# Attention scores in half-array F32R tiles, causal masks in the same halves, and a new schedule for the maximum pass

## The reference, cut to what matters

```
q = q * cos + rotate_half(q) * sin          # k likewise
scores = einsum('bhqd,bhkd->bhqk', q, k) / sqrt(16)
scores = where(causal, -inf, scores)
attn = softmax(scores)                      # maximum of each query is subtracted
out = einsum('bhqk,bhkd->bhqd', attn, v)
```

## Time and profile before

| what | us |
|---|---|
| device time, median of 3 runs | 2709.79 |
| span of the profiled execution, first to last instruction | 2663.3 |
| projection | 367.9 |
| routing | 44.8 |
| first two steps' maximum jobs | 23.5 |
| first pass of the attention loop | 852.7 |
| second pass | 858.1 |
| experts and dense | 516.0 |

### The profile page before, as it was taken

How to read it: one execution, slowest core, us unless ns; L and a number is a source line. 1 busy time by engine, 2 the same in 40 slices (tenths; PEclk the granted TensorE clock), 3 DMA queues, 4 the chain that set the end, 5 groups by cost and what they waited for, 6 DMA issues and landing times. The chain is left out here.

```text
span 2663.3 us, 49751 instructions
## 1 busy us (share of the span) xinstructions
PE 2394.4 (90%) x14968; PEld 1211.4 (45%) x14968; DVE 2072.5 (78%) x3856; ACT 1463.1 (55%) x1762; POOL 377.9 (14%) x319
## 2 busy tenths in 40 slices
PE   0999947999999999998899999999999868886998
PEld 0889942333333333232333333333322247776888
DVE  7888889999999988562799999988864257776776
ACT  2444513566666666777566666666677733332443
POOL 2111149500000000000000000000000023333344
PEclk9999977999999999999999999999999979998999
DMA  4122247300000021000410000003100144443232
GB/s 123 64 95 91 90 114 186 104 9 9 9 9 1 9 50 43 13 10 17 92 30 9 9 9 9 1 9 70 28 9 9 22 115 126 126 126 97 64 95 71
DMA packets 158629, 144.79 MB, mean 54 GB/s; under 512 B 36448, under 2 KB 142176, under 8 KB 158304
## 3 DMA queue, kind: packets, MB, share of 16 engines
q1 hardware_dynamic: 155360, 133.94, 18.9%
q0 software_dynamic: 3072, 8.39, 0.9%
HBM read 95.61 MB, written 46.66 MB: 53 GB/s over the span
## 5 line engine op out<-in xcount | busy, mean ns | idle before, releaser
L883 DVE TENSOR_REDUCE attn_MX<-psB 128x1 f32<-128x512 f32 (+3 forms) x2352 | 1357.2, 638 | 352.5 <-PE psB L756 223.2
L869 ACT ACTIVATE attn_PB<-psB 128x1024 f32<-128x1024 f32 (+3 forms) x1152 | 1035.8, 950 | 563.9 <-PE psB L788 509.7
L756 PE MATMUL psB<-attn_KS,attn_QS 96*128 96x512 bf16 (+3 forms) x2352 | 764.5, 370 | 51.5 <-DVE attn_MX L883 44.9
L788 PE MATMUL psB<-attn_QS,attn_KS 104*128 104x512 bf16 (+3 forms) x2304 | 652.6, 363 | 24.5 <-ACT attn_QS L846 16.0
L803 PE MATMUL psB<-attn_PB,attn_V 128*32 128x512 f32 (+3 forms) x4608 | 579.8, 570 | 0.0
L756 PEld LDWEIGHTS psB<-attn_KS,attn_QS 96*128 96x128 bf16 x2352 | 200.6, 97 | 639.8 <-DVE attn_MX L883 522.2
L788 PEld LDWEIGHTS psB<-attn_QS,attn_KS 104*128 104x128 bf16 x2304 | 210.2, 98 | 336.1 <-ACT attn_PB L869 128.9
L1043 POOL TENSOR_TENSOR W1L<-W,W1H 128x512 fp32r<-128x512 f32 x36 | 53.8, 1524 | 1664.3 <-ACT W1H L1120 1664.3
L803 PEld LDWEIGHTS psB<-attn_PB,attn_V 128*32 128x32 f32 x4608 | 96.3, 108 | 175.9 <-issue 166.8
L759 PE MATMUL psB<-attn_mask_qk,attn_idb 128*128 128x128 bf16 x544 | 119.2, 227 | 0.0
L42 PE MATMUL ps_experts<-W2H,HH_experts 128*128 128x256 f32 x256 | 83.9, 328 | 35.1 <-DVE Y_experts L1233 20.3
(11 more groups left out here) (213 smaller groups left out, 3216.5 us busy)
## 6 DMA issues: line engine op xcount, KB each, us to landing
W<-in_w SPq DMA_DIRECT2D x18, 1024.0 KB, 5.5
attn_KS<-qk_parts SPq DMA_DIRECT2D x240, 64.0 KB, 3.7
attn_QS<-qk_parts SPq DMA_DIRECT2D x210, 64.0 KB, 2.8
qk_parts<-proj_PT SPq DMA_DIRECT2D x32, 384.0 KB, 3.3
attn_V<-v_rows SPq DMA_DIRECT2D x40, 256.0 KB, 4.8
v_rows<-proj_VA SPq DMA_DIRECT2D x32, 256.0 KB, 2.0
XI_experts<-rows_by_place SPq DMA_DIRECT2D x9, 512.0 KB, 6.3
AO_experts<-attention_sums SPq DMA_DIRECT2D x9, 512.0 KB, 6.7
```

The source lines that it names most:

```text
L756: mm = nc.tensor.matmul(ps[:, bank, 0:width], QS[0:MROW, i % 4, h, j * P:(j + 1) * P], KS[w][0:MROW, h, kc * CH:kc * CH + width], start=Tr ...
L788: mm = nc.tensor.matmul(ps[:, bank, r * P:CH], KS[w][0:KROWS, h, kb * P:(kb + 1) * P], QS[0:KROWS, i % 4, h, r * P:CH], start=True, stop=( ...
L869: nc.scalar.activation(PB[:, u % RING, 2 * pair:2 * pair + 2, r * P:CH], ps[:, 2 * (s % 2):2 * (s % 2) + 2, r * P:CH], ACT.Exp, scale=HD * ...
L883: nc.vector.tensor_reduce(MX[:, m % 4, HG * j + h, kc:kc + 1], ps[:, MB + off % 3, 0:w], AX.X, ALU.max).then_inc(reduced, 1)
```

## The change

It changes these things and nothing else.

- **Parts.** q and k are cut into two F32R parts instead of three bf16 parts. Lines 277, 343 and 280 become one subtraction. `qk_parts` is [2, 512, 4096] float32.
- **Layout.** A head's contraction is 52 rows: high x high, high x low (16 rows each), 4 rows for the maximum, low x high. Heads 0 and 2 of a group lie in partitions 0 to 51, heads 1 and 3 in 64 to 115. The key and query tiles are F32R, with two heads on the free axis. All score products and maximum jobs run on 64 rows of the array; a score pair is one product in each half, into different banks.
- **Masks.** The mask product becomes two products of 64 columns for each head, 64 rows deep, in the head's own half (`later_qk`, `later_kq` times `hide`).
- **Maximum pass.** The diagonal jobs of the first two query blocks (one block in c = 0) take two heads at once into one bank, with one reduction. Diagonal jobs are issued in twos: both products, then the masks of both. A pass has 1092 jobs, 1152 before. `max_pass_pace` draws the smoothest line between the number of jobs that must be done and the number that may be done at each unit, and follows it.
- **Constants and loads.** The rows of ones come by 8 DMAs from a small tile instead of from GpSimd's 48 operations. A query load is 8 DMAs (two set the maximum rows to zero), before 6. SyncE waits for two small memsets first. `max_rows` has 8 small products, before 4.
- The first score pair of a step waits for both of ScalarE's `rows` copies.

```diff
-        PT = sb("PT", [P, 4, 3, CH], BF16)
-        RS = sb("RS", [P, 2, CH])
+        PT = sb("PT", [P, 4, 2, CH], F32R)
...
+                        dve.wait_ge(high_made, 4 * c + u + 1)
+                        nc.vector.tensor_tensor(PT[:, u, 1, :], ps[:, QTB + u % 2, :], PT[:, u, 0, :].bitcast(F32),
+                                                ALU.subtract).then_inc(low_made, 1)
...
-PAIRS = ((0, 0), (0, 1), (1, 0), (1, 1), (0, 2), (2, 0))
-MROW = HD * len(PAIRS)
-KROWS = MROW + 2 * HG
+TILE = P // 2
+MROW, MROWS = 32, 4
+TERMS = ((0, 0, 0), (HD, 0, 1), (MROW + MROWS, 1, 0))
+KROWS = HD * len(TERMS) + MROWS
...
+def diagonal_jobs(c):
+    paired = TPC // 2 if c > 0 else 1
+    wide = [(j, (t, t + 2), c) for j in range(paired) for t in range(2)]
+    return wide + [(j, (h,), c) for j in range(paired, TPC) for h in range(HG)]
...
-PACE = 4.5
-            room = min(room, 1.0) + PACE * (TPC - r) / TPC
-            while at < end(i + 1 + AHEAD) and room >= cost[at]:
...
+    path, at = [work[end(AHEAD)]], 0
+    while at < len(order):
+        low, high, low_at, high_at = float("-inf"), float("inf"), at, at
+        for to in range(at + 1, len(when)):
+            span = when[to] - when[at]
+            floor, roof = (work[least[to]] - path[at]) / span, (work[most[to]] - path[at]) / span
+            if floor > high or roof < low:
+                break
+            if floor >= low:
+                low, low_at = floor, to
+            if roof <= high:
+                high, high_at = roof, to
+        turn, slope = (high_at, high) if floor > high else (low_at, low)
+        path += [path[at] + slope * (when[to] - when[at]) for to in range(at + 1, turn + 1)]
+        at = turn
...
+                    for at, h in enumerate(hs):
+                        rows, b = slice(TILE * (h % 2), TILE * (h % 2) + KROWS), h // 2
+                        mm = nc.tensor.matmul(ps[:, bank, at * width:(at + 1) * width], QS[rows, i % 4, b, j * P:(j + 1) * P],
+                                              KS[w][rows, b, kc * CH:kc * CH + width], start=(at == 0), stop=(kc < c))
...
+                    both = jobs[i % LS][at:at + 2]
+                    for n, job in enumerate(both):
+                        max_job(reads, i, off + n, job, used(n), q_need)
+                    for half in range(2):
+                        for n, job in enumerate(both):
+                            mm = hide_later_keys(off + n, job, half)
+                            if half == 1:
+                                mm.then_inc(maxed, 1)
...
+                    for t in range(2):
+                        rows = slice(TILE * t, TILE * t + KROWS)
+                        mm = nc.tensor.matmul(ps[:, 2 * (s % 2) + t, r * P:CH], KS[w][rows, pair, kb * P:(kb + 1) * P],
+                                              QS[rows, i % 4, pair, r * P:CH], start=True, stop=(kb < TPC * c))
+                    if kb >= TPC * c:
+                        for half in range(2):
+                            for t in range(2):
+                                rows = slice(TILE * t, TILE * (t + 1))
+                                mm = nc.tensor.matmul(ps[:, 2 * (s % 2) + t, r * P + TILE * half:r * P + TILE * (half + 1)],
+                                                      later_kq[half][rows, :], hide[rows, 0, :], start=False, stop=(half == 1))

```

More of the change, by code:

```diff
@@ new lines, in max_pass_pace @@
+    when = [0.0] + list(itertools.accumulate((TPC - units[i][k][1]) / TPC for i, k in order))
+    least, most = [end(AHEAD)], [end(AHEAD)]
+    for i, k in order:
+        last = (i, k) == order[-1]
+        due = end(LS + AHEAD) if last else end(i + 2) if k >= len(units[i]) - 3 else 0
+        least.append(max(least[-1], due))
+        most.append(end(min(i + 1 + AHEAD, LS + AHEAD)))
+    path, at = [work[end(AHEAD)]], 0
[13 more added lines that the diff above has]
+        at = turn
@@ L587, in max_pass_pace @@
+    upto, count = [[] for _ in range(LS)], end(AHEAD)
+    for (i, k), goal, lo, hi in zip(order, path[1:], least[1:], most[1:]):
+        while count < hi and work[count + 1] <= goal + 0.5:
+            count += 1
+        count = max(count, lo)
+        upto[i].append(count)
     return upto
 def attend(nc, io, scratch, keep):
-    qk = scratch["qkp"].rearrange("s (w g h d) n -> s w g d h n", w=2, g=NG, h=HG)
+    qk = scratch["qkp"].rearrange("s (w g b t d) n -> s w g t d b n", w=2, g=NG, b=2, t=2)
@@ L602, in attend @@
     units = [key_blocks(c) for _, c in steps]
-    jobs = [[(j, h, kc) for kc in range(c + 1) for j in range(TPC) for h in range(HG)] for _, c in steps]
+    jobs = [[(j, (h,), kc) for kc in range(c) for j in range(TPC) for h in range(HG)] + diagonal_jobs(c) for _, c in steps]
     S_PER = sum(2 * len(u) + 1 for u in units)
```

238 lines of the change are left out of this document (116 added, 122 removed).

## The result

The changed kernel takes **2617.6 us** (median of six runs, 2607.6 to 2647.8) against 2709.5 beside it: a ratio of 0.967 [0.964, 0.970]. It is faster, as forecast, but by 92 us where 234 were predicted, and 2617.6 lies above the range's upper end of 2605. A ratio leaves out executions that took over 1.5% more than the kernel's shortest, a median takes them all.

The account below looks back on a forecast made before the run. TensorE was taken to bound attention, with VectorE next and nearly level in steps 1 to 7. From 2709.8 us, 214 for the two attention passes and 20 for routing were subtracted, giving 2476 us, range 2365 to 2605.

Parts of the forecast that it names:

- Steps 1 to 7: Attention steps with growing chunks: VectorE becomes the bound with 367 us, 386 with waits, against 434.8 before.
- the cheaper scores: Score products of the attention loop: pairs run together in two array halves, falling from 112 to 59 us in steps 1 to 7.
- Weight loads: F32R loads in attention: hidden in streams, uncovered only behind `weigh`, at most 52 us of TensorE's time; a third taken.
- Steps 9 to 15: Descending attention steps: TensorE 245 us with some jobs in twos, 270 us in all, against 307.9 before.
- Step 8: Middle step of an attention pass: TensorE 75 us against VectorE 64 and ScalarE 62, giving 76.5 us.
- Rival 1: Attention loop: coupling eats more, jobs never go in twos and bank waits delay scores; 797 us a pass, 2570 total; chance 0.22.
- Rival 4: Attention steps 9 to 15: the clock falls to 1.2 GHz, 245 us become 490, about 2960 in all; chance 0.03.
- if the clock falls in the loop: Attention loop: one of the listed signs that the prediction would be wrong; no size given.
- Routing: Stage before attention: VectorE's operations no longer stretched, loads some 5 us later but before VectorE is done; -20 us, between -10 and -22.
- 46.5 us around the span: Whole kernel: the difference between the 2663.3 us span and the 2709.8 us median, taken as unchanged.
- rival 3: Attention score pairs: the array halves do not overlap, a pair costs 0.454 us instead of 0.227; 2757 us total; chance 0.11.
- an estimate of 0.30 us for a pair: Attention scores: at 77% of the ideal packing, a pair costs about 0.30 us, the two passes some 30 us more.

Follow-up runs that it names:

- experiment 4: The changed kernel with GpSimd's 32 indirect transfers one at a time and the second key tensor's ones rows after the first key loads: 2575.7 us, 0.950.
- experiment 7: The kernel of experiment 4 with one or three full-array zero products ahead of each `weigh` but the first, steps 0, 1, 14, 15: 2569.6 and 2582.2 us.
- experiment 1: The changed kernel with GpSimd's sending of token rows held until the second group's key loads are done: 2620.6 us, ratio 0.969.

## Why the prediction was wrong

Against the sum of the prediction I hold the kernel of experiment 4, since stop and ones rows are priced apart. Its profiled execution is the longest of four, 7 us over their median, with the lowest clock. From the first to the last copy of the sums the sum gave 1482 us (732.5 and 749.5); 1627 were measured (794.3 and 832.9). Of the 145 us between them:

- **Steps 1 to 7, 39 us a pass: the failed step.** "VectorE is the bound with 367; with 1 us a step for the twos and some 12 for the waits, 386." Measured 425.0. VectorE was busy for 381.9, 15 over my 367: the sum by widths had come out 15.5 too low for before as well (382 against 397.5), and I wrote this down without carrying it over. The other 24 are waits: 43 us where I allowed 19. VectorE was busy for 90% of these steps, not for the 95 that I named as a sign. And it wasn't the bound alone: TensorE, for which the sum had 292 to 361, was busy for 403.0. Full arrays take 420.6 in the same steps with 413.1, so the cheaper scores, forecast to save 53 us of TensorE there, freed 10 of them and shortened nothing.
- **Weight loads: the term that was mis-sized.** "Uncovered they can only be behind `weigh`, once a unit: at most 0.09 us x 576 = 52 us [...] I take a third." I read them in the trace of experiment 4, pass 1. A product that waits for a bank or for ScalarE also starts together with its load. Two products that start together then cost 0.34 us instead of 0.23 (medians), a job in front of `weigh` 0.43 instead of the 0.32 with a load that is hidden. For the bf16 jobs of before the second difference is 0.01 (0.32 and 0.31). In steps 1 to 7 there are 424 such starts, 140 of them behind `weigh`; at 0.10 that is an estimate of 42 us, as much as TensorE lies above my 361. In part this is chance, as the same sum for before was 16 us under the busy time too (407 and 423.4). The cause is read from the starts; no run had half arrays with quick loads.
- **Steps 9 to 15, 19 us a pass.** I took 245 for TensorE, because some jobs go in twos, and let a third of the waits fall away. It is busy for 270.9 and idle for 18.3, exactly as much as before (307.9 less 289.6). By the starts in the trace the scores take 69 us where my sum had 46. Here 223 starts come together with their loads, 111 of them behind `weigh`: an estimate of 22 us at 0.10. Another 5 are the clock: step 15 takes 19.5 us at 0.50, 14.7 at 1.00 in pass 2 of the kernel with one product more (experiment 7).
- **Step 8, 3.7 us a pass**: 80.2 for 76.5; 67 such starts are 7 us, also an estimate.
- **Rival 1** named this coupling: 405 + 83 + 290 for the three stretches (by its own prices I get 402, 81 and 296, the same total), 425 + 80 + 289 measured. That its 2570 is near the 2575.7 of the kernel without the stop is luck: it starts from 2709.8, with the stop in it, and the kernel with the stop takes 2617.6; its pass is 797 us, 815.3 and 832.9 were measured.
- **Clock, some 20 us.** Rival 4 had named the clock, "a thin stream of products did not hold 2.4 GHz", but in the wrong place, and thin is not the whole of it: at 0.54 TensorE was busy for 89.0 of 89.5 us. What keeps it down is open. I looked for it in steps 9 to 15, which hold 1.00 nearly to the end; it fell in steps 14, 15, 0 and 1, where full arrays had held it (0.73 in step 0 before, 1.00 with the new schedule), and then stayed down into step 2. Steps 0 to 2 of pass 2 are 29 us longer than with full arrays. The chance of 0.03 was for a fall through a whole stretch of steps; the cheaper case I didn't list, though "if the clock falls in the loop" was one of my signs of being wrong. Its length is a matter of the execution: 129.7 us around the start of pass 2 in the changed kernel and in experiment 4, 41.0 in experiment 1.
- **Routing.** VectorE's part came out as forecast (done 21 us after the projection, small operations at 0.19). "SyncE has 8 loads for the ones ... some 5 us later, still before VectorE is done" is the failed sentence. They cost 2.04 each, not 0.46. That their source is one short row, read again and again, may be the reason; no run shows it, and the four that are left in front in experiment 4 cost 1.49 each. -7 in place of -20 in the change (first sums at 447.1 against 453.9); -17 to -18 with the rows moved, -14 in two other kernels that load them alike.
- **"46.5 us around the span."** Wrong: 2 us are there, the rest was a stop that this one execution lacked. It did no harm to the difference, as both kernels have the stop (38 and about 31 us), but a cause worth 1.4% stood outside my sum.

Right: score pairs start together and cost 0.23 (rival 3 fell); TensorE's busy time in steps 9 to 15 fell to 271; the projection's stage is unchanged (365.9 against 367.9 us); the first product behind `weigh` comes no later than before (1.00 then, 1.00 now), as its load runs beside it; the price is paid by the product behind that one. The sign was right, and for the wrong reason in part. More than half of the 92 us is the schedule's, which I had priced only through the job counts.

Two places of the Trainium skill beside this. Its figure in "TensorE: Matmul & The Clock Gate" (Part 3), from which I had worked out an estimate of 0.30 us for a pair, lies between the two prices measured, 0.23 with hidden loads and 0.34 without. And "TensorEngine Tiling (Array Packing)" (Tiling Modes, Key Properties) says that a change of the tiling mode drains TensorE. The trace agrees: a job whose load is hidden has its `weigh` 0.32 behind it, where in a stream of its own shape the next product comes after 0.23. The prediction left the rule out: the kernel before changes shape at each `weigh` too, and pays 0.31, so nothing seemed new, and nothing was.

## What to carry over

A wait between two engines that are both at 90% is not slack: before pricing a faster operation, find which engine the time of this stretch follows, and whether the other can use what is saved. Price a weight load not by a stream in which it is hidden, but by how often a product will have waited and starts together with it. And profile the kernel before more than once: where span and median differ, ask what the shown execution lacked.

## What was not expected of the hardware

- Taking work from TensorE slowed it: with half of the `weigh` left out, 2743 us for 2576, at a mean granted clock of 0.737 against 0.935, and TensorE busy throughout. Two full-array products of zeros a unit brought it back to 2587 and 0.941.
- 32 indirect transfers issued 1.27 us apart left TensorE, VectorE and ScalarE idle together for up to 14.8 us at a time in six of seven profiled executions, in step 1 or, sent later, in step 2; in the seventh (the first of the kernel before) they did not. Each behind the last one's landing, some 3 to 3.5 us apart, they stopped none. That is worth 38 us in the kernel before, as much as the half arrays with their routing and projection bring on top of the schedule.
- Eight DMAs that repeat a row of 512 bytes cost their queue 16.4 us, six plain ones 2.8.
- An F32R weight load of 0.19 us is free while it is hidden and costs some 0.10 us when its product has had to wait; a bf16 one of 0.10 us costs 0.01 then.
- At 1.2 GHz a stretch can be full of work (89.0 of 89.5 us busy) and stay there for 90 us; the same steps at a mean granted clock of 0.93 take 68.4. With `weigh` cut in two, steps 1 to 3 keep TensorE busy for 177.3 of 177.3 us at 0.50.
